# A fused recurrence and ternary feed-forward kernel: row scalings finished on GpSimd, the ternary sign in its own slot, transposes of the newest state tiles and the norms one slot later

## The reference

```python
# x: (16, 2048, 2048) fp32; W: (4096, 2048); w_fc: (5120, 2048); w_proj: (2048, 5120)
def attn(x, W, b):                       # a gated recurrence, not attention
    gates, values = split(einsum('btc,dc->btd', x, W) + b, 2)
    # hidden[t] = sigmoid(gates)[t] * hidden[t-1] + tanh(values)[t]
    return associative_scan(_scan_op, (sigmoid(gates), tanh(values)), axis=1)
def ternarize_weight(w):
    abs_mean = maximum(mean(abs(w)), 1e-05); thr = 0.7 * abs_mean
    return where(w > thr, 1, where(w < -thr, -1, 0)) * abs_mean
def ffn(x, w_fc, w_proj):
    h = square(relu(x @ ternarize_weight(w_fc).T))
    return h @ ternarize_weight(w_proj).T
x = x + layernorm(attn(layernorm(x), W, b))
x = x + layernorm(ffn(layernorm(x), w_fc, w_proj))
```

## Time and profile before

| | |
|---|---|
| median of 3 runs | 3162.07 us |
| the profiled execution (its slowest core's span) | 3165.74 us (3164.2 us, core 6) |
| spans of the 8 cores | 3122.0 to 3164.2 us |
| TensorE / VectorE / ScalarE / GpSimd busy in core 6 | 95% / 54% / 43% / 10% |
| core 6, scan stage: first product of the next stage starts at | 1131.78 us |

### The profile page before, as it was taken

One profiled execution on the slowest core, in us unless ns is written; L12 is line 12 of the kernel. 1 busy time (PEld: TensorE's weight loads), 2 busy tenths in 40 slices (PEclk: granted clock), 3 DMA queues, 4 the chain that ended last, 5 costly groups with the idle time before them and its releaser, 6 DMA issues.

```text
span 3164.2 us, 53790 instructions; the slowest of 8 cores (3122.0 to 3164.2 us)
## 1 busy us (share of the span) xinstructions
PE 2999.3 (95%) x20660; PEld 2046.6 (65%) x20660; DVE 1713.7 (54%) x2472; ACT 1345.8 (43%) x2118; POOL 303.9 (10%) x454
## 2 busy tenths in 40 slices
PE   3899898999899999999999999999999999999997
PEld 2788787888788864868678676685444444444443
DVE  2355445667666638523567676741554454454454
ACT  2435555444444456667566666653111111111111
POOL 0011111111111111111011111110000000000000
PEclk8999999999999999999999999999999999999999
DMA  7968787777776879365565746618333233333231
GB/s 227 306 203 249 232 267 223 222 225 224 229 243 204 239 256 271 119 191 142 155 163 161 189 145 181 182 40 303 132 130 107 103 122 122 103 122 114 97 126 68
DMA packets 303806, 564.59 MB, mean 178 GB/s; under 512 B 150080, under 2 KB 196288, under 8 KB 289472
## 3 DMA queue, kind: packets, MB, share of 16 engines
q1 hardware_dynamic: 267680, 401.74, 43.0%
q0 software_dynamic: 35872, 159.40, 14.4%
HBM read 372.85 MB, written 154.66 MB: 167 GB/s over the span
## 4 chain that ended last, share of the span: by engine, by line
PE 71%; DMA 8%; DVE 7%; SPq 6%; issue 4%; ACT 4%; POOL 0%; DVEq 0%; ACTq 0%; POOLq 0%
PE psA L112 44%; PE psB L112 27%; SPq L108 6%; DMA slab<-wfc 5%; DVE st L100 2%; DVE xr L120 1%; ACT xn L92 1%; PE psB L144 1%; DMA slab<-wpj 1%; DMA xr<-x 1%; DVE qst L120 1%; DMA xnT<-xn 1%; DMA slab<-W 1%; DVE hTr L140 1%; DVE q L136 1%
## 5 line engine op out<-in xcount | busy, mean ns | idle before, releaser
L112 PE MATMUL psA<-xnT,wt 128*128 128x256 bf16 x8192 | 947.3, 279 | 69.1 <-DMA xnT<-xn 38.9
L112 PEld LDWEIGHTS psA<-xnT,wt 128*128 128x128 bf16 x8192 | 818.6, 100 | 182.1 <-issue 72.3
L112 PE MATMUL psA<-xn1T,wq 128*128 128x512 bf16 (+1 forms) x2560 | 436.7, 329 | 1.7 <-ACT zb L92 1.4
L140 DVE TENSOR_TENSOR_SCAN hTr<-gt,hTr 128x256 f32<-128x256 f32 x248 | 183.4, 742 | 337.6 <-ACT hTr L92 337.2
L112 PEld LDWEIGHTS psA<-xn1T,wq 128*128 128x128 fp8e4 x2560 | 250.6, 98 | 174.2 <-issue 2.4
L112 PE MATMUL psB<-w,hs 128*128 128x512 fp8e4 x1600 | 349.9, 379 | 0.0
L112 PE MATMUL psA<-w,hs 128*128 128x512 fp8e4 x1600 | 349.9, 379 | 0.0
L112 PEld LDWEIGHTS psB<-w,hs 128*128 128x128 bf16 x1600 | 156.6, 98 | 188.8
L112 PEld LDWEIGHTS psA<-w,hs 128*128 128x128 bf16 x1600 | 156.5, 98 | 188.8
L112 PE MATMUL psB<-xn1T,wq 128*128 128x256 bf16 (+1 forms) x1776 | 275.3, 313 | 2.8 <-DVE xn1T L136 2.8
L112 PEld LDWEIGHTS psB<-xn1T,wq 128*128 128x128 fp8e4 x1776 | 174.9, 99 | 91.8 <-issue 6.6
(11 more groups left out here) (82 smaller groups left out, 3417.1 us busy)
## 6 DMA issues: line engine op xcount, KB each, us to landing
slab<-wfc SPq DMA_DIRECT2D x160, 512.0 KB, 6.6
slab<-wpj SPq DMA_DIRECT2D x160, 512.0 KB, 4.7
pc<-h_s SPq DMA_DIRECT2D x64, 640.0 KB, 5.8
h_s<-hst_b POOLq DMA_DIRECT2D x140, 256.0 KB, 3.1
xr<-x POOLq DMA_DIRECT2D x32, 1024.0 KB, 9.5
x_s<-xr POOLq DMA_DIRECT2D x32, 1024.0 KB, 7.0
xb<-x_s SPq DMA_DIRECT2D x64, 512.0 KB, 4.7
xin<-x SPq DMA_DIRECT2D x31, 1024.0 KB, 7.6
```

Source lines behind the costliest of these rows:

```text
L112: return lambda e: e.matmul(*a, **k)
L140: return lambda e: e.tensor_tensor_scan(*a, **k)
```

## The change

Four things change together.
1. `scaling` replaces the two copies of the statistics. VectorE negates the mean right after the statistics, and GpSimd multiplies it with rs right after the power, so `ln_norm` and `n3` leave nothing to VectorE.
2. A ternary step's sign (ScalarE) and is_gt/min (VectorE) fall in one slot: the sign before the slot's product, is_gt/min after its scan. The next slab load is issued on SP ahead of the previous store. The slots are 1, 2, 6, 9, 10, 13, 14, 15 (before: 1, 5, 6, 9, 12 to 15), with a second step in 6 and 9 (before: 5 and 9). The first slab's two-operation form on VectorE goes.
3. The newest state tiles of row tile 0 are transposed one slot later.
4. The parts s, t, q and n of `Back` move one slot later, but for s1, which stays at 7. x1's load moves from 7 to 8, x0's to the end of the pass before.

```diff
+        def scaling(n, st, src, t_in):
+            mv, ve, rs, nm = sm[f"mv{n}"], s1[f"ve{n}"], s1[f"rs{n}"], s1[f"nm{n}"]
+            for j in range(4):
+                t = DVE.do(op.bn_stats(...), t_in)
+            t = DVE.do(op.bn_aggr(mv, st[:, :]), t, free[f"mv{n}"])
+            DVE.do(op.tensor_scalar(out=ve, in0=mv[:, 1:2], scalar1=EPS, scalar2=None, op0=ALU.add), t)
+            t = DVE.do(op.tensor_scalar(out=mv[:, 0:1], in0=mv[:, 0:1], scalar1=-1.0, scalar2=None, op0=ALU.mult), t)
+            t = POOL.do(op.tensor_tensor(out=rs, in0=ve, in1=mhalf[:, :], op=ALU.pow), t, t_half, free[f"nm{n}"])
+            t = POOL.do(op.tensor_tensor(out=nm, in0=mv[:, 0:1], in1=rs, op=ALU.mult), t)
+            free[f"mv{n}"] = t
+            return t
...
         def ln_norm(src, t, out=None):     # likewise Back.n3
-            t = DVE.do(op.scalar_tensor_tensor(out=s1["nm1"][:, :], ...), t_rs, free["rs1"])
             t = ACT.do(op.activation(out=xn[:, :], ..., bias=nm1, scale=rs1), t, free["xn"])
...
         for n in range(len(srcs)):         # tern_pass
-            if done is not None:
-                store(n - 1, done)
             while len(ahead) < min(3, len(srcs) - n):
                 ahead.append(slab_load(srcs[n + len(ahead)]))
             i, t = ahead.pop(0)
+            t = lower(n, i, t)
+            if done is not None:
+                store(n - 1, done)
-            t = DVE.do(op.scalar_tensor_tensor(... is_gt, min), low)
-            slab_free[i] = done = t
             half[0] = True
             yield
             half[0] = False
-            if ahead:
-                low = lower(n + 1, *ahead[0])
+            slab_free[i] = done = DVE.do(op.scalar_tensor_tensor(... is_gt, min), t)
             yield
...
-        BACK = {0: "x0", 2: "s0", 3: "t0", 4: "q0", 6: "n0", 7: "x1 s1", 10: "t1", 11: "q1", 13: "n1"}
+        BACK = {3: "s0", 4: "t0", 5: "q0", 7: "s1 n0", 8: "x1", 11: "t1", 12: "q1", 14: "n1"}
...
-                    trans(k, 0, range(11) if j == 13 else [j - 3])
+                    trans(k, 0, {13: range(9), 14: (9, 10), 15: (11,)}[j])
```

More of the change, by code:

```diff
@@ L309, in build_program @@
         free = {"xin": None, "xn": None, "nm1": None, "rs1": None, "rs2": None,
-                "xn3": None, "nm3": None, "rs3": None, "xr": None, "rs4": None, "sc4": None, "bs4": None}
-        def ln_stats(src, t_in):
[L313 to L327, removed]
+                "xn3": None, "nm3": None, "mv1": None, "mv3": None, "xr": None, "rs4": None, "sc4": None, "bs4": None}
@@ L328, in ln_norm @@
+        def ln_stats(src, t_in):
+            return scaling(1, st1, src, t_in)
+        def ln_norm(src, t, out=None):
+            free["nm1"] = t = ACT.do(op.activation(
+                out=(xn if out is None else out)[:, :], in_=src[:, :], func=AF.Identity,
+                bias=s1["nm1"], scale=s1["rs1"]), t, free["xn"] if out is None else None)
             return t
@@ L392, in abs_pass, with tern_pass @@
                 yield
-        def tern_pass(srcs, thr, nthr, dst, marks, share):
+        def tern_pass(srcs, thr, dst, marks):
             phase[0] = "tern"
@@ L401, in lower @@
             def lower(n, i, t):
[L402 to L406, removed]
+                return ACT.do(op.activation(out=qst[n % 3][:, :], in_=stage[i], func=AF.Sign, scale=1.0 - 2.0 ** -24,
+                                            bias=thr, saturate=False), t, q_free[n % 3])
             def store(n, t):
                 q_free[n % 3] = marks[n] = SP.dma(d_q[n % 3], op.dma_start(out=dst(n), in_=qst[n % 3][:, :]), t)
-            low = done = None
+            done = None
             for n in range(len(srcs)):
-                if done is not None:
-                    store(n - 1, done)
                 while len(ahead) < min(3, len(srcs) - n):
@@ L433, in tern_pass @@
                 half[0] = False
-                if ahead:
-                    low = lower(n + 1, *ahead[0])
+                slab_free[i] = done = DVE.do(op.scalar_tensor_tensor(
+                    out=qst[k][:, :], in0=stage[i], scalar=thr, in1=qst[k][:, :],
+                    op0=ALU.is_gt, op1=ALU.min, saturate=False), t)
                 yield
@@ L661, in s3 @@
             def s3(self, tt):
[L662 to L668, removed]
+                self.t[tt] = scaling(3, st2, self.buf[tt], self.t[tt])
             def n3(self, tt):
                 row, buf = self.k * TA + tt, self.buf[tt]
-                t = DVE.do(op.scalar_tensor_tensor(
-                    out=s1["nm3"][:, :], in0=sm["mv3"][:, 0:1], scalar=-1.0, in1=s1["rs3"][:, :],
-                    op0=ALU.mult, op1=ALU.mult), self.t[tt], free["rs3"])
                 t = ACT.do(op.activation(out=xn3[:, :], in_=buf[:, :], func=AF.Identity,
-                                         bias=s1["nm3"][:, :], scale=s1["rs3"][:, :]), t, free["xn3"])
-                free["nm3"] = free["rs3"] = t
+                                         bias=s1["nm3"][:, :], scale=s1["rs3"][:, :]),
+                           self.t[tt], free["xn3"])
+                free["nm3"] = t
                 free["xn3"] = xh_mark[row] = POOL.dma(d_xh, op.dma_start(out=xh_d[row], in_=xn3[:, :]), t)
@@ L1132, in build_program @@
                     step(ROWS)
-                twice = phase[0] == "tern" and j in (5, 9)
+                twice = phase[0] == "tern" and j in (6, 9)
                 if phase[0] != "tern":
                     step(PREP, (k, j) > (2, 0))
-                elif j in (1, 5, 6, 9, 12, 13, 14, 15):
+                elif j in (1, 2, 6, 9, 10, 13, 14, 15):
                     step(PREP)
@@ L1147, in build_program @@
             back = Back(k)
+            back_do(back, "x0")
         drain(PREP)
```

25 lines of the change are left out of this document (8 added, 17 removed).

## The result

The changed kernel takes 3140.61 us (median of 12 runs), the kernel before 3164.19 us (median of 12) beside it: a ratio of 0.9929, 95% interval 0.9902 to 0.9957. It is faster by 0.7%. The forecast was 3114 us, 1.5%. The direction and the range hold; less than half of the forecast gain arrived. The ratios leave out executions in which the cores of one die ran longer at a lower granted clock; the medians do not.

The account below looks back on a forecast made before the run. TensorE was taken as the bound, stopping mainly at transposes into `psB`. Savings 33 + 7 + 12 - 1 = 51 us gave 3115 from 3165.7, 3111 for the median, plus 3 for core spread: 3114 us; range 3090 to 3148 (8 in 10).

Parts of the forecast that it names:

- nm on GpSimd: 64 scalings move to GpSimd, 0.6 to 1.3 us each, hidden in every slot; only the kernel's start loses 1 us.
- Passes 3 to 6: The |w| passes, 271 us: 3 us saved a pass, 12 us in all (bounds -2 and 30).
- Pass 7: Pass of 71 us with TensorE idle for 7.9: 7 us saved (0 to 10).
- rival B: Nearly all stops go, |w| passes drop to 61 us too: 3087 us, chance 0.11.
- Slack of the norms one slot later: Room left before the transposes: 0.7 us at slot 13, 1.0 us at slot 5; later slabs show fully.
- rival A: Stops return under another name, `psB` freed late at slots 13 and 5: 3148 us, chance 0.18.
- The ternary step in one slot: Slab loads can go out at least 10.8 us before their sign; seven ternary passes save 33 us (0 to 47).
- the 59.6 us pass: Ternary pass without stops: measured 66.3 us less 4.7 of waits and 2.0 of slow clock.
- The rivals: Four other outcomes beside the forecast (chance 0.60): 3148, 3087, 3185 and 3162 us.
- D: No change, 3162 us: slab supply alone sets a pass's length and stops only move; chance 0.06.
- C: Slower, 3185 us: part t a slot late at slots 4 and 11, 22 us over 13 passes; chance 0.05.
- the prediction's own signs: No 2.6 us `hTr` wait at slot 13, short norm and sign waits, ternary passes 60 to 63 us, clock 0.98.

Follow-up runs that it names:

- e4: Changed kernel with xin's load behind the transposing DMA on SP's queue instead of ahead of it: 0.9775 of the kernel before, median 3094.83 us.
- e18: Changed kernel with xin's load behind the transposing DMA, repeated beside the change on one chip: 0.9777 of the kernel before, 3098.59 us.
- e1: Kernel before with only part 1 of the change (nm on GpSimd): 0.9973 of the kernel before.
- e3: Kernel before with only parts 3 and 4 (transposes and norms one slot later): 0.9986 of the kernel before, no change.
- e2: Kernel before with only part 2 (ternary sign and is_gt/min in one slot, new slots): 0.9966 of the kernel before.
- e9: Changed kernel without part 1 (nm stays on VectorE): 1.016 of the kernel before, slower.
- e13: Kernel before with parts 1 and 2, without 3 and 4, and xin's load behind the transposing DMA: 0.9888 of the kernel before.

## Why the prediction was wrong

By its own steps:

- *nm on GpSimd*, nothing on the path and ScalarE's waits taken away: right. The multiplication, which the trace of before did not show, has a record of 0.19 us, below my 0.6 to 1.3. On core 6, GpSimd's two operations in a row:

```profile
684.54 0.88 POOL L136 TENSOR_TENSOR s<-s,mhalf 128x1 f32<-128x1 f32 x1 [1.78 <-DVE sm L132]
685.56 0.19 POOL L136 TENSOR_TENSOR s<-sm,s 128x1 f32<-128x1 f32 x1
```

  GpSimd's power beside two scans again takes longer, 0.88 us, as in the earlier trace rows (0.84), and core 6's scans average 740 ns in the ternary passes of both kernels. The rule of the Trainium skill (SBUF — State Buffer, "Who interferes with whom") in its other direction, a scan held up by GpSimd, cost nothing that the trace shows; leaving it out of the sum was right.
- *Passes 3 to 6*: 12.6 us against 12. *Pass 7*: 4.1 against 7. Both near. The forecast read core 6 alone, whose |w| passes took 67.7 us where the mean core's took 65.5; on core 6 they went to 64.2, near my 64.7, in the mean to 62.4, on the way to rival B's 61.
- *Slack of the norms one slot later*, 0.7 and 1.0 us: right in kind. The `xr` waits are 18.5 us on core 6, under the 25 us set for rival A. A's time (3148) is near the measured one, but its mechanism carries only part of it: with xin's load behind, `xr` waits fall to 7.8 us with the same slack.
- *The ternary step in one slot*, the term of 33 us (bounds 0 and 47): **this step failed.** It says "Now a second slab load stands ahead of xin and the transpose", and draws from it only that the sign's slab comes in time. TensorE's wait for the transposing DMA itself, `xnT`, it puts at nothing without a reason: it never asks when that DMA lands, beside what, and for whom. The runs showed 22.2 us of `xnT` waits per core in its place (2.3 before), and the term measured 6.5 us. With the one reordered load the ternary passes take 421.4 us (e4) and 421.2 (e18) where the kernel before takes 458.2, 36.8 us less, 60.2 us per pass against the predicted 60 to 63. So the working of the 59.6 us pass, and the price of the stops removed, held.
- *The rivals*: none names `xnT`. It was absent from the waits in the earlier trace rows: the late norm sent that DMA out when its slab load had landed and the store of x1 was half done, and TensorE's own stops at slot 13 (2.1 and 2.55 us) gave it more time. What is shown is that the wait appears with part 1 alone (35.1 us, e1) and also with parts 3 and 4 alone (16.1 us, e3), and goes with xin's place (e4, e18). Part 2, where the prediction saw the second slab load, brings none of it by itself (0.8 us, e2).

The sum itself has a slip that decides nothing: a tenth of A and all of D lie within 0.2%, which makes 0.08 and leaves C's 0.05 for slower, where the prediction has 0.06 and 0.07.

Against the prediction's own signs: the `hTr` wait is gone, and so is "ACT xn <- DVE s", though 19.9 us on GpSimd in eight waits are more than "little". The sign still waits long (16.8 us, but for a store, not for a slab). Of the rest of TensorE's waits only half is named `xr`. The ternary passes take 64.5 us and not 60 to 63, and the granted clock in them is 0.97 on core 6 and not 0.98.

Open: how the 17 to 26 us of one landing divide among slab loads, xin and GpSimd's store of x1. Only xin's place was tried by itself; the store moved only along with other parts (e9, e13). And why part 2, and parts 3 and 4, spread the cores beside the slow DMA.

## What to carry to other kernels

Before pricing the removal of a stop, list every transfer that starts earlier once the stop is gone, what then stands ahead of it in its queue, and how long it has until its reader. A transfer that shows no wait may be covered by the very stop that you remove. Look at the other queues too: what else will be in flight at its new time. In one queue, put the small transfer that someone waits for ahead of the large one that has a whole pass of time: here that is one swapped pair of lines, and it is worth about twice the change itself (1.5 points against 0.7).

## What the runs showed of the hardware

- What the landing of the same transposing DMA depends on: the loads of SP's queue in flight when it is issued, and when GpSimd's 1 MB store of x1 is issued. All such DMAs between 560 and 1060 us, eight cores, of the twenty traces of this study; time from issue to landing in us, as minimum / median / maximum, and how many:

| in flight ahead | store 1 us before to 4 us after | 4 to 6 us after | at another time |
|---|---|---|---|
| xin, two slab loads | 10.9 / 15.9 / 24.1 (193) | 11.2 / 16.0 / 26.5 (170) | 7.2 / 8.5 / 14.0 (55) |
| xin, one slab load | 10.0 / 17.2 / 25.3 (200) | 7.4 / 11.8 / 21.2 (24) | 6.9 / 8.9 / 15.0 (559) |
| xin | 9.7 / 11.2 / 19.6 (60) | 6.7 / 8.3 / 16.1 (60) | 7.0 / 8.5 / 12.0 (202) |
| two slab loads | 5.4 / 12.1 / 19.8 (86) | 5.6 / 6.9 / 12.9 (201) | 5.2 / 6.6 / 8.4 (51) |
| one slab load | 4.6 / 6.4 / 11.1 (58) | 4.3 / 5.0 / 5.9 (26) | 5.0 / 5.9 / 8.6 (177) |
| none | 5.2 / 5.9 / 6.7 (12) | 4.3 / 4.4 / 7.0 (110) | 4.4 / 5.7 / 7.7 (75) |

  With the store at another time the DMA lands within 15.0 us whatever is ahead. With loads ahead and the store issued while it is in flight it takes up to 26.5 us. So xin's load behind seems to help in two ways: less is ahead, and the DMA is nearly through when the store comes. This is read from kernels that differ in other things too; no run moves the store alone.
- The same kernel gained 0.3% on one chip and 0.7 to 0.8% on two others (intervals 0.9949 to 0.9991, 0.9902 to 0.9957, 0.9902 to 0.9944). Differences under half a point between kernels need one chip.
